# Causal mask of a maxima pass: added by a matrix product on TensorE, or by VectorE inside its maximum

## The chip, the cores and the metric

The kernel runs on one core of a Trainium2 chip. The metric is the device time of one execution in microseconds, as the median of several runs. The engines are called by their short names: PE is TensorE (PEld its weight loads), DVE VectorE, ACT ScalarE, POOL GpSimd, SP SyncE with its DMA queue (SPq).

## What is computed

The reference is one transformer decoder layer in float32, for 2 batches of 1024 tokens, 256 channels, 16 heads of 16 channels, and a context of 77 tokens:

```python
xn1 = _ln(x, g1, be1)
sa = _mha(xn1, xn1, Wq_s, bq_s, Wk_s, bk_s, Wv_s, bv_s, causal=True)
x = x + (sa @ W1 + b1)
xn2 = _ln(x, g2, be2)
ca = _mha(xn2, encoder_out, Wq_c, bq_c, Wk_c, bk_c, Wv_c, bv_c, causal=False)
x = x + (ca @ W2 + b2)
xn3 = _ln(x, g3, be3)
ff = jax.nn.relu(xn3 @ Wf1 + bf1) @ Wf2 + bf2
return x + ff
```

In `_mha` the scores are `q k^T / scale` with `scale = DH ** -0.5`, so they are multiplied by 4. In the causal attention the scores above the diagonal are set to minus infinity ahead of the softmax.

## The kernel before

**Stages.** The kernel normalizes x in four pieces of 512 rows, projects them to q, k and v, splits q and k into three bf16 parts each and stores these in DRAM. Then come the causal attention, its output product, the projection of the second q, the cross attention, its output product and the feed-forward part. This case is about the causal attention, some 65 to 350 us into the run.

**Groups.** The 2 x 16 heads are taken four at a time: 8 groups (NG), each with GH = 4 heads of one batch. A group goes through two passes over its scores.

**The maxima pass** finds the largest score of each query row, so that the exponential can be shifted. For a tile t of 128 queries the keys 0 to 128(t+1) are taken in chunks of up to 512 columns (`a.chunks`, a list of t, first head, number of heads, first key, width w). A chunk fills one PSUM bank of 512 float32 columns: four heads where w is 128, two where it is 256, one where it is 384 or 512. There are 38 chunks in a group. 22 of them hold the diagonal of their tile (`diagonal`, L906): 1, 2, 4 and 4 chunks for the widths 128, 256, 384 and 512, once for the tiles 0 to 3 and once more, from key 512 on, for the tiles 4 to 7. They hold 32 heads between them. PE fills a chunk with one matmul per head (L911). On a diagonal chunk a second matmul per head (L915) adds the mask to the last 128 columns: an identity in bf16 times `maskb`, which holds zeros and -1e30. DVE takes the maximum of each head with one reduce for the chunk (L1141) into `max_a`, or into `max_b` for keys from 512 on, and at the end of a group the larger of the two (L1146). POOL negates the 32 maxima per row and splits them into three bf16 parts (L600 to L609), PE transposes them (L922), DVE copies them to `shift_t` (L1154), and SP loads them as three further rows of the q stack (L428).

**The score pass.** PE computes the scores anew, transposed, and with the shift rows as part of the contraction (L948). ACT takes the exponential (L732), POOL zeroes the block above the diagonal (L617), and PE multiplies with v and a column of ones (L973; one product per step of key tiles). ACT copies the sums out and stores them, SP loads heads and sums back after every second group, DVE inverts the sums (L1169), SP spreads the inverses, and DVE multiplies (L1177).

**What sets the order.** Every engine runs its own list in order. `Attention.order` spreads the maxima chunks of a group between the score units of the group before it (`lead=1.35`: chunks are 1.35 groups ahead), so PE goes through chunks, score units, products and transposes in one list, `a.pe`, and the other engines follow the same list. The chunks rotate through three PSUM banks (`M_BANKS`): PE waits before chunk `use` until DVE has read chunk `use - 3` (`max_read`), DVE waits for `max_full`. The score units have three more banks, which ACT frees. The first 14 entries are run before the last projection, the next 30 are spread between its parts and the projection of the context.

Of the kernel before, what the change touches and what calls it, by code (L numbers as in the profile page):

```python
# [19 lines left out]
ALU = mybir.AluOpType  # L20
# [6 lines left out]
P = 128  # L27
# [167 lines left out]
def build(nc, x, w_qkv, w_ctx, w_mid, w_f1, w_f2, ctx_t, cols, rows, out):  # L195
# [12 lines left out]
    with ExitStack() as ctx:  # L208
        def sb(name, shape, dt=F32):
            return ctx.enter_context(nc.sbuf_tensor(name, shape, dt))  # L210
# [8 lines left out]
        row = sb("row", [P, 5, C])  # L219
        identf = sb("identf", [P, P])  # L220
        identb = sb("identb", [P, P], BF16)
        maskb = sb("maskb", [P, P], BF16)
        neghalf = sb("neghalf", [P, CT])

        arena_h = sb("arena_h", [P, NG // 2 * T])
# [16 lines left out]
        v_ctx = sb("v_ctx", [S_CTX, NG, GW])  # L242
        wf1_high = sb("wf1_high", [P, KC, FF], F32R)
        wf1r = (wf1_high[:, :, :], wf1_low[:, :, :])

        v_group = sb("v_group", [P, 3, TILES, GH, 32])
        out_t = sb("out_t", [P, T])
# [279 lines left out]
        def _(pool):  # L527
            c = [0]

            def made(ins, n=1):  # L530
                ins.then_inc(consts, 1)
                c[0] += 1
            made(pool.memset(identf[:, :], 0.0))
            made(pool.memset(identb[:, :], 0.0))
            made(pool.memset(maskb[:, :], 0.0))
            made(pool.memset(neghalf[:, :], -0.5))
            pool.wait_ge(consts, 4)
            for m in (identf, identb):
                made(pool.affine_select(out=m[:, :], in_=m[:, :], compare_op=ALU.not_equal, fill=1.0, base=0,
                                        pattern=[[-1, P]], channel_multiplier=1))  # L540
            made(pool.affine_select(out=maskb[:, :], in_=maskb[:, :], compare_op=ALU.is_ge, fill=NEG, base=0,
                                    pattern=[[-1, P]], channel_multiplier=1))

            def ln_root(k):

# [265 lines left out]
        def _(pe):  # L811
# [84 lines left out]
            def attention(a, s, lo, hi=None):  # L896

                def k_rows(n, g, h, lo, hi):
                    return (k_self[0:n, g % a.nb, h, lo:hi] if a.causal else k_ctx[0:n, g, h, lo:hi])

                def chunk(use, g, c):

                    t, h0, nh, s0, w = a.chunks[c]
                    if c == 0:
                        pe.wait_ge(s.q_in[g % a.nb], 16 * len(QP) * (1 + a.causal) * (g // a.nb + 1))
                        if g == 0 and not a.causal:  # L906
                            pe.wait_ge(s.k_in, 16 * len(KP))
                    diagonal = a.causal and s0 + w == (t + 1) * P
                    for h in range(h0, h0 + nh):
                        o = (h - h0) * w  # L910
                        ins = nc.tensor.matmul(m_bank(use)[:, o:o + w],  # L911
                                               q_stack[0:ROWS, g % a.nb, h, t * P:(t + 1) * P],
                                               k_rows(ROWS, g, h, s0, s0 + w), start=True, stop=not diagonal)
                        if diagonal:
                            ins = nc.tensor.matmul(m_bank(use)[:, o + w - P:o + w], identb[:, :], maskb[:, :],  # L915
                                                   start=False, stop=True)
                    return ins

                def shift_rows(use, g):
# [156 lines left out]
        def _(dve):  # L1076
# [55 lines left out]
            def attention(a, s, lo, hi=None):  # L1132

                def chunk(use, g, c):
                    t, h0, nh, s0, w = a.chunks[c]
                    p = g % 2
                    if c == 0:
                        at_least(dve, s.shift_step, 5 * (g - 2) + 1)
                        at_least(dve, s.maxima, g - 1)
                    dst = max_b[:, p, h0:h0 + nh, t - 4:t - 3] if s0 else max_a[:, p, h0:h0 + nh, t:t + 1]  # L1140
                    nc.vector.tensor_reduce(dst, m_bank(use)[:, 0:nh * w].rearrange("p (h w) -> p h w", h=nh),  # L1141
                                            AX.X, ALU.max).then_inc(s.max_read, 1)
                    if c + 1 == len(a.chunks):
                        dve.wait_ge(s.max_read, use + 1)
                        late = max_a[:, p, :, 4:8]
                        nc.vector.tensor_tensor(late, late, max_b[:, p, :, :] if a.causal else late, ALU.max)\  # L1146
                            .then_inc(s.maxima, 1)

                def shift_rows(use, g):
                    if g:  # L1150

                        dve.wait_ge(s.shift_in[(g - 1) % a.nb], 16 * PARTS * ((g - 1) // a.nb + 1))
                    src = m_bank(use).bitcast(BF16)[0:PARTS * GH * TILES, 0:P]
                    nc.vector.tensor_copy(shift_t[:, :], src).then_inc(s.max_read, 1)  # L1154

                def rows(use, n, half):

                    norm = (NCH if a.causal else 2 * NCH) + n
                    dve.wait_ge(bias_added, norm - NCH + 1)
                    add_half(m_bank(use).rearrange("p (j c) -> p j c", c=C), n, half).then_inc(s.max_read, 1)  # L1160
                    if half:
                        dve.wait_ge(s.max_read, use + 1)
                        ln_sums(norm)

                def invert_sums(g):
                    if g % 2 == 0:
                        return
                    dve.wait_ge(s.heads_in, 32 * (g // 2 + 1))
                    nc.vector.reciprocal(sums[:, :], sums[:, :]).then_inc(s.recips_done, 1)  # L1169

                def divide_heads(g):

                    if g % 2 == 0:
                        return
                    dve.wait_ge(s.recips_in, 16 * (g // 2 + 1))
                    o = heads_out[:, g // 2, :]
                    nc.vector.tensor_tensor(o, o, recips[:, :], ALU.mult).then_inc(s.heads_done, 1)  # L1177

                for op, *what in a.pe[lo:hi]:
                    if op == "score" and a.behind("inverted", *what) is not None:  # L1180
                        invert_sums(a.behind("inverted", *what))
                    if op == "score" and a.behind("divided", *what) is not None:
                        divide_heads(a.behind("divided", *what))
                    if op == "norm":
                        ln_apply((NCH if a.causal else 2 * NCH) + what[0])
                    if op != "m":
                        continue
                    use = what[0]
                    kind, *of = a.uses[use]
                    dve.wait_ge(s.max_full, use + 1)  # L1190
                    {"chunk": chunk, "shift": shift_rows, "rows": rows}[kind](use, *of)
                return invert_sums, divide_heads
# [10 lines left out]
            for n in range(3):  # L1203
                for u in range(4):
                    split(4 * n + u)
                add_v(n)
                if n == 0:
                    dve.wait_ge(x_in[3], 16)
                    ln_sums(3)
                    ln_apply(3)  # L1210
            attention(SELF, S1, 0, SELF_EARLY[0])
            for u in range(4):
                attention(SELF, S1, SELF_EARLY[u], SELF_EARLY[u + 1])
# [104 lines left out]
```

## Time and profile before

| | |
|---|---|
| median of 3 runs | 627.89 us |
| range of the runs | 627.78 to 629.59 us |
| span of the profiled execution | 631.5 us |
| busy share, PE / DVE / ACT / POOL | 80% / 58% / 49% / 30% |
| instructions, PE / DVE | 3296 / 695 |

The profile comes from an execution of its own, whose span stands in the table beside the timed runs. A busy share is an average over stages with different limits. The duration of a matmul is pipelined: its end overlaps the next one, so what a matmul costs is read from the distance of two starts. The same holds, to a lesser degree, for DVE.

### The profile page before, as it was taken

How to read it: one execution, taken by the hardware profiler on the slowest of the kernel's cores; microseconds unless marked ns; L12 is line 12 of the kernel's file. 1: busy time of each engine (PE TensorE's matmuls, PEld its weight loads, DVE VectorE, ACT ScalarE, POOL GpSimd, SP SyncE). 2: the span in 40 equal slices, each digit the busy share in tenths (PEclk: the TensorE clock that was granted, in tenths of full speed). 3: DMA queues.
4: the chain of work that ended last, by engine and by line, in shares of the span. 5: the costliest groups of instructions: out<-in, count | busy, mean ns of one | idle time of the engine just before them, and what ended most of it. 6: DMA issues, size and time to landing. Idle time of an engine off the chain costs nothing.

```text
span 631.5 us, 8807 instructions
## 1 busy us (share of the span) xinstructions
PE 504.7 (80%) x3296; PEld 296.2 (47%) x3296; DVE 368.2 (58%) x695; ACT 307.5 (49%) x590; POOL 187.8 (30%) x276
## 2 busy tenths in 40 slices
PE   1775775999997999799988835669576757989887
PEld 0664452344443444344333333434222446988877
DVE  4887697678886788678532147645221763454430
ACT  3544020667765776477666502247443535253460
POOL 3788821131221132122132523305131350121200
PEclk9988697799999999899999969767555968999998
DMA  8138936007367335727260266978333212101001
GB/s 288 47 109 158 201 116 118 0 21 116 52 120 105 67 66 107 115 56 38 83 186 1 68 168 92 173 108 140 107 99 115 81 47 72 34 0 34 18 17 34
DMA packets 41930, 56.51 MB, mean 89 GB/s; under 512 B 12832, under 2 KB 27424, under 8 KB 41888
## 3 DMA queue, kind: packets, MB, share of 16 engines
q1 hardware_dynamic: 39584, 47.56, 38.1%
q10 hardware_dynamic: 2304, 8.39, 3.8%
q8 instruction: 26, 0.43, 0.3%
q14 instruction: 16, 0.13, 0.1%
HBM read 35.12 MB, written 20.42 MB: 88 GB/s over the span
## 4 chain that ended last, share of the span: by engine, by line
PE 44%; DMA 23%; DVE 15%; ACT 6%; SPq 5%; issue 3%; POOL 2%; ACTq 0%; DVEq 0%
PE ps L864 10%; PE ps L973 9%; PE ps L948 8%; PE ps L911 7%; DMA arena_h<-heads 6%; DMA stacks<-shift_t 6%; PE ps L1060 5%; DMA recips<-recip_rows 4%; DVE max_a L1141 4%; ACT arena_p L732 4%; DMA heads<-out_t 4%; DVE xn L1094 3%; SPq L409 2%; PE ps L933 2%; SPq L428 2%
## 5 line engine op out<-in xcount | busy, mean ns | idle before, releaser
L732 ACT ACTIVATE arena_p<-ps 128x512 f32<-128x512 f32 (+4 forms) x416 | 190.9, 541 | 129.5 <-PE ps L948 127.3
L1141 DVE TENSOR_REDUCE max_a<-ps 128x1 f32<-128x512 f32 (+4 forms) x280 | 159.6, 620 | 46.6 <-PE ps L911 34.0
L948 PE MATMUL ps<-stacks 99*128 99x512 bf16 (+2 forms) x448 | 149.9, 369 | 27.6 <-DMA stacks<-shift_t 22.5
L911 PE MATMUL ps<-stacks 96*128 96x77 bf16 (+4 forms) x640 | 146.2, 306 | 32.1 <-DVE max_a L1141 19.1
L911 PEld LDWEIGHTS ps<-stacks 96*128 96x128 bf16 x640 | 58.9, 111 | 97.5 <-DVE max_a L1141 45.5
L973 PE MATMUL ps<-arena_p,v_group 128*32 128x512 f32 (+4 forms) x896 | 94.1, 540 | 0.7 <-POOL arena_p L617 0.5
L617 POOL TENSOR_SCALAR_AFFINE_SELECT arena_p<-arena_p 128x512 f32<-128x512 f32 x64 | 41.0, 653 | 169.9 <-ACT arena_p L732 169.9
L948 PEld LDWEIGHTS ps<-stacks 99*128 99x128 bf16 (+1 forms) x448 | 45.6, 107 | 93.1 <-ACT arena_p L732 37.8
L1141 DVE TENSOR_REDUCE max_b<-ps 128x1 f32<-128x384 f32 (+3 forms) x88 | 52.5, 636 | 21.3 <-PE ps L915 21.3
L864 PE MATMUL ps<-wf2r,hid_r 128*128 128x256 f32 x384 | 49.9, 294 | 9.6 <-DVE hid_r L1254 9.6
L864 PEld LDWEIGHTS ps<-wf2r,hid_r 128*128 128x128 f32 x384 | 49.1, 202 | 10.7 <-DVE hid_r L1254 10.7
L1121 DVE TENSOR_TENSOR xs<-ps,xs 128x512 f32<-128x512 f32 x24 | 16.4, 690 | 63.7 <-PE ps L864 44.7
L915 PE MATMUL ps<-maskb,identb 128*128 128x128 bf16 x256 | 51.9, 228 | 0.0
L1060 PE MATMUL ps<-xn_r,wf_high 128*128 128x512 f32 x128 | 42.3, 413 | 10.6 <-DVE xn_r L1247 10.6
L798 ACT ACTIVATE hid_r<-ps,col 128x512 fp32r<-128x512 f32 x32 | 22.1, 689 | 58.8 <-PE ps L1060 55.6
L571 POOL TENSOR_TENSOR parts<-arena_p,parts 128x512 bf16<-128x512 f32 (+1 forms) x26 | 32.2, 1239 | 39.2 <-DVE parts L1106 39.2
L717 ACT ACTIVATE arena_p<-ps,col 128x512 f32<-128x512 f32 (+1 forms) x26 | 17.3, 666 | 52.6 <-PE ps L848 43.2
L562 POOL TENSOR_TENSOR xs<-xs,row 128x256 f32<-128x256 f32 x48 | 38.6, 836 | 9.2 <-DVE xn L1094 9.2
L973 PEld LDWEIGHTS ps<-arena_p,v_group 128*32 128x32 f32 (+1 forms) x896 | 23.8, 112 | 36.2 <-issue 30.1
L1094 DVE TENSOR_SCALAR xn<-xs,mean_var,rstd 128x256 f32<-128x256 f32 x48 | 29.6, 678 | 16.7 <-POOL rstd L550 16.7
L1254 DVE TENSOR_TENSOR hid_r<-arena_p,hid_r 128x512 fp32r<-128x512 f32 x32 | 23.2, 731 | 19.8 <-ACT arena_p L801 19.8
L1104 DVE TENSOR_TENSOR arena_p<-arena_p,parts 128x512 f32<-128x512 f32 (+1 forms) x26 | 20.4, 785 | 24.0 <-issue 16.9
(68 smaller groups left out, 528.1 us busy)
## 6 DMA issues: line engine op xcount, KB each, us to landing
heads<-out_t ACTq DMA_DIRECT2D x16, 512.0 KB, 4.3
stacks<-q_parts SPq DMA_DIRECT2D x48, 128.0 KB, 5.2
stacks<-k_parts SPq DMA_DIRECT2D x48, 128.0 KB, 7.6
stacks<-qc_parts SPq DMA_DIRECT2D x48, 128.0 KB, 5.1
arena_h<-heads SPq DMA_DIRECT2D x8, 512.0 KB
recips<-recip_rows SPq DMA_DIRECT2D x8, 512.0 KB
q_parts<-parts SPq DMA_DIRECT2D x8, 384.0 KB, 2.5
k_parts<-parts SPq DMA_DIRECT2D x8, 384.0 KB, 2.6
```

The source lines that it names most:

```text
L562: ins = pool.tensor_tensor(xt, xt, row[:, r, :], ALU.add)
L571: pool.tensor_tensor(p[:, 2, :], rest[:, u % 2, 0:width], p[:, 1, :], ALU.subtract)\
L617: pool.affine_select(out=blk, in_=blk, compare_op=ALU.is_ge, fill=0.0, base=0, pattern=[[0, GH], [1, P]], channel_multiplier=-1).then_inc( ...
L732: nc.scalar.activation(probs[0:a.kp, a.probs_slot(g, ui), h, k * BANK:k * BANK + width], ps[0:a.kp, unit % S_BANKS, 0:width], ACT.Exp, sca ...
L864: ins = nc.tensor.matmul(acc[:, j, :], lhs_t(k, j), rhs(k), start=(k == 0), stop=(k == n_k - 1))
L911: ins = nc.tensor.matmul(m_bank(use)[:, o:o + w], q_stack[0:ROWS, g % a.nb, h, t * P:(t + 1) * P], k_rows(ROWS, g, h, s0, s0 + w), start=T ...
L915: ins = nc.tensor.matmul(m_bank(use)[:, o + w - P:o + w], identb[:, :], maskb[:, :], start=False, stop=True)
L948: ins = nc.tensor.matmul(ps[0:keys, unit % S_BANKS, lo - k * BANK:hi - k * BANK], k_rows(ROWS_S, g, h, i * P, i * P + keys), q_stack[:, g ...
L973: ins = nc.tensor.matmul(out_region[32 * h:32 * h + 32, lo:hi], v, probs[0:a.kp, slot, h, o:o + hi - lo], start=(i == 0), stop=last, skip_ ...
L1060: ins = nc.tensor.matmul(ps[:, 2 + u % 4, :], wf1r[hw][:, kc, f * P:(f + 1) * P], xn_r[:, hx, k % 2, kc, :], start=(i == 0), stop=(i == le ...
L1094: nc.vector.tensor_scalar(xn[:, p, j, :], xs[:, n * CT + j, :], mean_var[:, p, j, 0:1], rstd[:, p, j:j + 1], ALU.subtract, ALU.mult).then_ ...
L1141: nc.vector.tensor_reduce(dst, m_bank(use)[:, 0:nh * w].rearrange("p (h w) -> p h w", h=nh), AX.X, ALU.max).then_inc(s.max_read, 1)
```

## The change

The two matmuls per diagonal head become one. DVE reads the scores of one head from the bank and, from SBUF, a row of `w` mask values whose last 128 columns hold the triangle and whose others are zero. One fused instruction adds the two, writes the sum back to the bank and keeps the running maximum, which goes to `max_a` or `max_b`. There is one such instruction for each head of a diagonal chunk; the 16 other chunks of a group keep their single reduce. The semaphore `max_read` is raised by the last head of a chunk.

The mask is now float32, 128 x 512, and lies in the first 512 columns of `wf1_high`, a tile for the feed-forward weights that POOL fills near the end of the cross attention, long after the last causal chunk. POOL fills it with zeros at the start and writes the triangle into its last 128 columns. DVE waits once for these constants before its first chunk.

```diff
-        maskb = sb("maskb", [P, P], BF16)
...
+        mask_r = wf1_high[:, 0, 0:BANK]
+        mask = mask_r.bitcast(F32)
...
-            made(pool.memset(maskb[:, :], 0.0))
+            made(pool.memset(mask, 0.0))
...
-            made(pool.affine_select(out=maskb[:, :], in_=maskb[:, :], compare_op=ALU.is_ge, fill=NEG, base=0,
-                                    pattern=[[-1, P]], channel_multiplier=1))
+            made(pool.affine_select(out=mask_r[:, BANK - P:BANK], in_=mask[:, BANK - P:BANK], compare_op=ALU.is_ge,
+                                    fill=NEG, base=0, pattern=[[-1, P]], channel_multiplier=1))
...
-                    diagonal = a.causal and s0 + w == (t + 1) * P
...
-                                               k_rows(ROWS, g, h, s0, s0 + w), start=True, stop=not diagonal)
-                        if diagonal:
-                            ins = nc.tensor.matmul(m_bank(use)[:, o + w - P:o + w], identb[:, :], maskb[:, :],
-                                                   start=False, stop=True)
+                                               k_rows(ROWS, g, h, s0, s0 + w), start=True, stop=True)
...
-                    nc.vector.tensor_reduce(dst, m_bank(use)[:, 0:nh * w].rearrange("p (h w) -> p h w", h=nh),
-                                            AX.X, ALU.max).then_inc(s.max_read, 1)
+                    if a.causal and s0 + w == (t + 1) * P:
+
+                        for j in range(nh):
+                            ins = nc.vector.tensor_tensor_reduce(
+                                out=m_bank(use)[:, j * w:(j + 1) * w], in0=m_bank(use)[:, j * w:(j + 1) * w],
+                                in1=mask[:, BANK - w:BANK], scale=1.0, scalar=NEG, op0=ALU.add, op1=ALU.max,
+                                accum_out=dst[:, j, :])
+                        ins.then_inc(s.max_read, 1)
+                    else:
+                        nc.vector.tensor_reduce(dst, m_bank(use)[:, 0:nh * w].rearrange("p (h w) -> p h w", h=nh),
+                                                AX.X, ALU.max).then_inc(s.max_read, 1)
...
+            dve.wait_ge(consts, 7)
             attention(SELF, S1, 0, SELF_EARLY[0])
```

In the compiled program each fused instruction is two instructions of DVE: the pass itself and a read of its accumulator. This is DVE's list at the start of the causal attention, before (a row is a line, an operation, out<-in, the shape of the output and how often it repeats):

```order
L1114 TENSOR_TENSOR arena_v<-ps,row 128x4x64 x4
L1141 TENSOR_REDUCE max_a<-ps 128x4
L1141 TENSOR_REDUCE max_a<-ps 128x2 x2
L1141 TENSOR_REDUCE max_a<-ps 128x1 x12
L1141 TENSOR_REDUCE max_b<-ps 128x4
```

and in the changed kernel, where `wf_high` is the tile with the mask:

```order
L1111 TENSOR_TENSOR arena_v<-ps,row 128x4x64 x4
L1141 ISA ps,max_a<-ps,wf_high 128x128
L1141 ISA max_a 128x1
L1141 ISA ps,max_a<-ps,wf_high 128x128
L1141 ISA max_a 128x1
```

The one reduce of the first chunk has become four pairs, one per head. In the whole program DVE's list has 256 pairs in the place of 176 reduces.

On PE, at the same place (the end of the v projection and the first two chunks, for each of four heads), before:

```order
L864 MATMUL ps<-wqkv_r,xn_r 128x256 x24
L911 MATMUL ps<-stacks 128x128
L915 MATMUL ps<-maskb,identb 128x128
L911 MATMUL ps<-stacks 128x128
L915 MATMUL ps<-maskb,identb 128x128
```

and in the changed kernel:

```order
L865 MATMUL ps<-wqkv_r,xn_r 128x256 x24
L911 MATMUL ps<-stacks 128x128 x4
L911 MATMUL ps<-stacks 128x256 x4
L911 MATMUL ps<-stacks 128x384 x4
L911 MATMUL ps<-stacks 128x512 x7
```

The masks between the heads are gone, and with them the weight load of the identity and the weight load back to q, 256 times in the program. The order of everything else is the same on every engine.

## Rows read from the trace of the kernel before

**Rows 1.** The page: busy time, share and instructions of each engine.
```profile
PE 504.7 (80%) x3296; PEld 296.2 (47%) x3296; DVE 368.2 (58%) x695; ACT 307.5 (49%) x590; POOL 187.8 (30%) x276
```

**Rows 2.** Windows: length, busy us per engine (count), granted clock, DMA share, GB/s.
```profile
67.97:93.65 25.68, 21.42 (x117) 12.81 (x116) 24.98 (x46) 5.06 (x8) 12.79 (x5) 0.90 0.71 152
121.83:149.86 28.03, 28.00 (x227) 12.31 (x226) 22.54 (x42) 19.98 (x46) 6.72 (x14) 1.00 0.35 52
189.72:207.88 18.16, 14.30 (x109) 6.13 (x107) 12.13 (x20) 10.33 (x21) 2.74 (x5) 0.91 0.77 112
207.88:251.54 43.66, 43.52 (x346) 19.16 (x345) 35.05 (x63) 30.63 (x71) 10.70 (x24) 1.00 0.39 78
211.51:273.30 61.79, 57.64 (x452) 25.37 (x451) 47.10 (x84) 40.63 (x91) 13.44 (x28) 0.97 0.50 87
```

**Rows 3.** Chain of waits, 165 to 285 us: start, us, what.
```profile
183.16 6.54 DMA arena_h<-heads
...
193.66 7.77 DMA stacks<-shift_t
```

**Rows 4.** Waits of 120 to 322 us: total us, times, longest.
```profile
PEld ps L911 <- DVE max_a L1141: 16.4, 43, 0.8
```

**Rows 5.** Timeline of the plain group, PE's product, then DVE: start, us, engine, operation.
```profile
121.83 1.92 PE L973 MATMUL ps<-arena_p,v_group 128*32 128x512 f32 x16
...
124.11 1.02 DVE L1141 TENSOR_REDUCE max_b<-ps 128x1 f32<-128x384 f32 x2 [1.31 <-PE ps L915]
125.06 2.48 DVE L1141 TENSOR_REDUCE max_a<-ps 128x1 f32<-128x512 f32 x4
...
129.23 1.89 DVE L1141 TENSOR_REDUCE max_b<-ps 128x1 f32<-128x512 f32 x3 [1.10 <-PE ps L915]
131.15 0.18 DVE L1146 TENSOR_TENSOR max_a<-max_a,max_b 128x16 f32<-128x16 f32 x1
...
133.78 1.02 DVE L1141 TENSOR_REDUCE max_a<-ps 128x1 f32<-128x384 f32 x2 [0.64 <-PE ps L915]
...
138.48 1.89 DVE L1141 TENSOR_REDUCE max_a<-ps 128x1 f32<-128x512 f32 x3 [0.82 <-PE ps L915]
141.59 1.29 DVE L1141 TENSOR_REDUCE max_a<-ps 128x1 f32<-128x512 f32 x2 [1.22 <-PE ps L911]
...
146.23 1.29 DVE L1141 TENSOR_REDUCE max_b<-ps 128x2 f32<-128x512 f32 x2 [0.35 <-PE ps L915]
```

**Rows 6.** Groups by form: operation, shapes, count, busy us, mean ns, idle before.
```profile
L1141 DVE TENSOR_REDUCE max_a<-ps 128x1 f32<-128x512 f32 x160 | 100.7, 682 | 17.7 <-PE ps L911 12.6 <-PE ps L915 5.0
...
L915 PE MATMUL ps<-maskb,identb 128*128 128x128 bf16 x256 | 51.9, 228 | 0.0
...
L1141 DVE TENSOR_REDUCE max_b<-ps 128x1 f32<-128x384 f32 x32 | 16.2, 550 | 9.2 <-PE ps L915 9.2
```

**Rows 7.** Timeline of PE in that group: first of eight, and the next after.
```profile
130.13 0.22 PE L911 MATMUL ps<-stacks 96*128 96x128 bf16 x1
...
130.60 0.22 PE L948 MATMUL ps<-stacks 99*128 99x128 bf16 x1
```

**Rows 8.** Timeline of PE in the first chunk, a mask and what follows.
```profile
67.19 0.31 PE L915 MATMUL ps<-maskb,identb 128*128 128x128 bf16 x1
67.30 0.31 PE L911 MATMUL ps<-stacks 96*128 96x128 bf16 x1
```

**Rows 9.** Timeline of DVE, its smallest operations back to back; their group by form.
```profile
20.16 0.38 DVE L1085 BATCH_NORM_AGGREGATE mean_var<-stats 128x2 f32<-128x6 f32 x4
...
L1085 DVE BATCH_NORM_AGGREGATE mean_var<-stats 128x2 f32<-128x6 f32 x48 | 4.6, 157 | 0.4
```

**Rows 10.** Timeline of DVE and of SP's queue at the first shift rows.
```profile
102.07 0.21 DVE L1154 COPY shift_t<-ps 96x128 bf16<-96x128 bf16 x1
...
104.04 1.88 SPq L428 DMA_DIRECT2D stacks<-shift_t  x3
```

**Rows 11.** Timeline of POOL: its first work after the constants.
```profile
6.30 0.23 POOL L547 TENSOR_SCALAR veps<-mean_var 128x4 f32<-128x4 f32 x1 [2.63 <-DVE mean_var L1085]
```

## The prediction

> **What bounds the kernel now.** I first read the engine line of the page [rows 1]: PE 80%, DVE 58%. That average decides nothing, because the change touches only the causal attention, so I went to the windows of that stretch [rows 2]. They say three things. In the first chunks (67.97 to 93.65 us) DVE is busy 24.98 of 25.68 us: DVE sets the pace. In a plain group (121.83 to 149.86 us) PE is busy 28.00 of 28.03 us and DVE 22.54. Every second group is longer: 211.51 to 273.30 us is a pair of groups, 61.79 us, with 5.7 us more than two plain ones. I cut such a pair into a stall stretch (189.72 to 207.88 us in the pair before, 18.16 us) and a long stretch (207.88 to 251.54 us, 43.66 us, DVE busy 35.05). The chain of waits [rows 3] shows the stall stretch: a load of heads ends at 183.16 + 6.54 = 189.70 us, DVE must invert sums from it before it comes to the copy of the shift rows, the load of these rows takes 7.77 us, and PE scores again only when it has ended, at 193.66 + 7.77 = 201.43 us.
>
> So PE bounds the plain groups, with DVE at 80% behind it. The two are tied by three banks: in the waits of 120 to 322 us PE's chunk loads stand 16.4 us behind DVE's reduces [rows 4]. The DVE timeline of the plain group shows the other side [rows 5]: six waits for PE, 1.31, 1.10, 0.64, 0.82, 1.22 and 0.35 us, 5.44 in all. The PE row above them shows why: 16 product matmuls from 121.83 us take 1.92 us, PE fills no bank meanwhile, and DVE had 0.97 us of reduces left (it ran dry at 124.11 - 1.31 = 122.80 us).
>
> **What is removed.** A batch-head group has 8 x 4 = 32 diagonal heads, so 256 mask matmuls go, as many as the group table counts [rows 6]. Its 228 ns is a pipelined duration; from the start of the first to the end of eight such matmuls of 128 columns, four of them masks, go 130.60 - 130.13 = 0.47 us [rows 7], a step of 0.058 us. That is 32 x 0.058 = 1.86 us of PE per group, 14.9 us in all, and 0.11 us each where the granted clock is at its lower level [rows 8]. Also gone are the 22 reduces per group that read diagonal chunks.
>
> **What is added.** 32 fused passes per group, each two DVE instructions (the pass and a read of the accumulator). The elements stay: the same widths are read. What changes is the overhead per instruction. Four reduces of 512 take 2.48 us [rows 5], one lasts 0.682 [rows 6], so they start every (2.48 - 0.682) / 3 = 0.599 us. The forms of 384 and 512 differ by 0.682 - 0.550 us for 128 elements, about 1.04 ns each; 512 take 0.533 us of the step, and **0.066** is overhead. A group now pays 22 x 0.066 = 1.45 us for this.
> The pair's overhead, c, is in no row. Bounds: the four aggregates of 6 elements start every (0.38 - 0.157) / 3 = 0.074 us [rows 9]; if pass and read overlap like neighbours, c = 0.066 + 0.074 = **0.14**. If the read starts only after the pass has ended, as the small maximum at 131.15 does (0.03 us after the reduces' end at 129.23 + 1.89), c = 0.150 + 0.03 + 0.074 = **0.25** (0.150 is 0.682 less 0.533). Nothing excludes the low end and no semaphore stands between the two, which speaks for it; but the accumulator is whole only when the pass has gone through the pipe. I take half of that tail, **0.18**: per group 32 x 0.18 - 1.45 = +4.3 us of DVE.
>
> **The sum.** (1) First 16 heads, DVE bound: 16 x 0.18 - 11 x 0.066 = +2.15; the first reduce starts four mask matmuls earlier at the low clock, -0.43: **+1.7**. (2) Next 14 heads, among projections that also use DVE, before 95 us: 14 x 0.18 - 9 x 0.066 = **+1.9**. (3) Twelve heads before the shift copy at 102.07 us: +1.7, but the copy is over by 102.28 and SP issues the row loads only at 104.04, after the loads of the next stacks [rows 10]: 1.76 us of cover, **0**. Without that cover it would be +1.7. (4) A plain group: DVE 22.54 + 4.3 = 26.8 us, plus what is left of its waits. Where DVE is the later one, three full banks stand before it when a product starts: 3 x (1.02 - 0.55 + 0.115) = 1.75 us instead of 0.97, so 1.31 becomes 0.53 (0.115 is 0.18 - 0.066 a head); the other five, in the same way, about 0.56, 0.2, 0, 0.57, 0. Together 28.7 to 28.8 us against 28.03: **+0.75**, two groups **+1.5**. PE's saved 1.86 us is spent waiting for DVE. (5) A long stretch: 52 diagonal heads, 35 old reduces, 35.05 + 52 x 0.18 - 35 x 0.066 = 42.1, and 2.9 of waits, 45.0 against 43.66: +1.4; in its stall stretch two heads before the copy and four at the low clock: +0.3. Two pairs: **+3.4**. (6) The rest (111.56 to 121.83, and the last chunks behind 301.33 us): **+0.6**. Sum **+9.1 us**.
> At no cost: POOL fills 128x512 instead of 128x128, but it then stood idle 2.63 us for DVE's first statistics [rows 11]. The mask lies in a weight tile that is written after the last chunk. The new wait for constants on DVE is met 60 us before. ACT and the other DMAs keep their work and follow PE.
>
> A rule speaks against the change. The rows show reduces that start 0.599 us apart and last 0.682, so neighbours overlap by 0.083 us [rows 5, 6]. The Trainium skill, VectorE: DVE Perf Modes, "The DRAIN you can't avoid", says that the next operation waits until the pipe is empty. These rows do not bear that out for plain reduces; for the pair they cannot tell. What it would give is a rival below. The same page, "Two Vector instructions with no wait between them", counts an operation with an accumulator output as two instructions and holds neither when all operands start in the same quadrant of partitions, as here; by that the sum would be that of c = 0.14, and no run here shows it yet.
>
> **Rivals.** *Cheap pair, no net change.* c = 0.14: (1)+(2) +2.5, plain groups -0.5 each, pairs -0.6 each, total about 0: **628**. *Faster.* DVE stays off the path: the waits of rows 5 hide the added work, and PE cashes its matmuls: two plain groups -3.7, two long stretches with 52 masks -6.0, start +2.5: **621**. For it: 5.44 us of DVE idle per group, as much as is added. Against: they lie behind products, not spread out. It decides for c under about 0.155. *Costly pair.* c = 0.25: (1) to (3) +6.5, plain +3.0 each, pairs +5.6 each, rest +0.9: **652**. *Nothing overlaps.* The pass costs its whole duration and the read its own, c = 0.150 + 0.157 = 0.31: (1) to (3) +9.1, plain groups +9.8, pairs +17.8, rest +1.2: **666**. That is the time that the page's rule on the pipe gives. *Half speed.* The fused pass takes two cycles an element: 10,240 diagonal elements a group, 10.7 us more DVE in each: over **700**. Reduce and two-input operations both run one a cycle here, so little speaks for it.
>
> **How the numbers follow.** The sum is made against one profiled execution with a span of 631.5 us, 3.6 over the median of the runs, 627.89; the difference carries over: 627.9 + 9.1 = **637**. Chances: forecast (c 0.16 to 0.22) 0.46, costly 0.12, nothing overlaps 0.04, half speed 0.02, together 0.64 slower; cheap pair 0.17; faster 0.19. A measurement here tells 0.3%, 1.9 us, from no change. The forecast's own range is 631 to 645; with cases of both signs the range is 620 to 654, about one in ten outside it at either end.
>
> **What would show it.** In the changed profile: accumulator reads of about 0.07 to 0.16 us, and the step of a pair less its elements is c. If I am right DVE is busy about 27 of some 28.8 us in a plain group, its waits for PE shrink below 2.5 us, and PE's waits for DVE grow. DVE near 25 us and a group under 27.5 would prove me wrong towards faster; a c over 0.22 towards slower. If the start (to about 102 us) is not 3 to 4 us later, terms (1) and (2) are wrong.

## The result and the profile after

The changed kernel takes 636.05 us (median of 4 runs, 635.16 to 641.26), the kernel before, measured beside it, 628.74 (4 runs, 627.78 to 632.33). The ratio is 1.0133 [1.0067, 1.0199] (in brackets the 95% interval): slower, by 0.7 to 2.0%. A later comparison of the two (c_after below) gave 1.0102 [1.0046, 1.0158] (637.31 against 632.09 us). Ratios are formed from undisturbed runs, so they are not always the quotient of the medians beside them. Single runs of one kernel scatter by 5 us and more (the kernel before ran in 625.68 to 637.61 us on one chip), so what follows rests on lengths of stretches. The plain groups of a kernel repeat to 0.01 us and its start to 0.1 us; the stretch ahead of the first product and the stalled groups repeat less well, and are told with their scatter.

The profiled execution has a span of 633.5 us; its page:

```profile
span 633.5 us, 8632 instructions
...
PE 505.8 (80%) x3040; PEld 280.7 (44%) x3040; DVE 383.7 (61%) x1031; ACT 308.7 (49%) x590; POOL 187.7 (30%) x276
```

256 instructions less on PE, 336 more on DVE, and DVE's busy time is up by 15.5 us from 368.2 [rows 1]. The windows of the changed kernel, the first chunks up to the first projection matmul and the plain group, with the columns of [rows 2]:

```profile
66.22:74.42 8.20, 7.03 (x20) 2.00 (x20) 7.44 (x33) 0.00 (x0) 8.20 (x1) 0.50 1.11 237
123.40:151.86 28.46, 27.42 (x195) 10.09 (x194) 24.63 (x83) 20.31 (x45) 6.69 (x14) 1.00 0.36 52
```

And the same first stretch of the kernel before:

```profile
66.90:74.35 7.45, 7.03 (x35) 3.59 (x36) 6.38 (x12) 0.00 (x0) 7.45 (x1) 0.59 1.11 237
```

The plain group went from 28.03 to 28.46 us, DVE in it from 22.54 to 24.63 us, PE from 28.00 to 27.42. All four plain groups of the program have the same length, to 0.01 us, before and after. DVE's timeline of that group, its beginning and its waits for PE:

```profile
123.43 0.55 DVE L1141 CUSTOM_DVE_ANT_0 ps<-ps,wf_high 128x384 f32<-128x384 f32 x1
123.91 0.14 DVE L1141 DVE_READ_ACCUMULATOR2_ANT max_b<- 128x1 f32 x1
123.91 0.60 DVE L1141 CUSTOM_DVE_ANT_0 ps<-ps,wf_high 128x384 f32<-128x384 f32 x1
124.42 0.14 DVE L1141 DVE_READ_ACCUMULATOR2_ANT max_b<- 128x1 f32 x1
125.63 0.57 DVE L1141 CUSTOM_DVE_ANT_0 ps<-ps,wf_high 128x384 f32<-128x384 f32 x1 [1.07 <-PE ps L911]
...
130.69 0.70 DVE L1141 CUSTOM_DVE_ANT_0 ps<-ps,wf_high 128x512 f32<-128x512 f32 x1 [0.92 <-PE ps L911]
...
140.01 0.70 DVE L1141 CUSTOM_DVE_ANT_0 ps<-ps,wf_high 128x512 f32<-128x512 f32 x1 [0.36 <-PE ps L911]
...
143.12 1.29 DVE L1147 TENSOR_REDUCE max_a<-ps 128x1 f32<-128x512 f32 x2 [1.21 <-PE ps L911]
...
148.00 0.43 DVE L1141 CUSTOM_DVE_ANT_0 ps<-ps,wf_high 128x256 f32<-128x256 f32 x1 [0.24 <-PE ps L911]
```

Two things are to be seen. An accumulator read (0.14 us) starts at the same time as the next pass (both at 123.91): it does not hold that pass back. And the five waits are 1.07, 0.92, 0.36, 1.21 and 0.24 us, 3.80 in all, where [rows 5] had 5.44. How fast pairs follow each other is plain in the first chunk of 128 columns, four heads without a wait:

```profile
67.20 0.14 DVE L1141 DVE_READ_ACCUMULATOR2_ANT max_a<- 128x1 f32 x1
67.20 0.33 DVE L1141 CUSTOM_DVE_ANT_0 ps<-ps,wf_high 128x128 f32<-128x128 f32 x1
...
67.45 0.33 DVE L1141 CUSTOM_DVE_ANT_0 ps<-ps,wf_high 128x128 f32<-128x128 f32 x1
...
67.70 0.33 DVE L1141 CUSTOM_DVE_ANT_0 ps<-ps,wf_high 128x128 f32<-128x128 f32 x1
67.94 0.14 DVE L1141 DVE_READ_ACCUMULATOR2_ANT max_a<- 128x1 f32 x1
```

One pair every 0.248 us (67.20 to 67.45 to 67.70 us). The groups by form say what each part lasts:

```profile
L1147 DVE TENSOR_REDUCE max_a<-ps 128x1 f32<-128x512 f32 x128 | 80.9, 682 | 12.4 <-PE ps L911 12.3
...
L1141 DVE CUSTOM_DVE_ANT_0 ps<-ps,wf_high 128x512 f32<-128x512 f32 x64 | 43.1, 717 | 8.6 <-PE ps L911 8.6
...
L1141 DVE DVE_READ_ACCUMULATOR2_ANT max_b<- 128x1 f32 x128 | 18.0, 140 | 0.0
...
L1141 DVE CUSTOM_DVE_ANT_0 ps<-ps,wf_high 128x128 f32<-128x128 f32 x64 | 16.6, 322 | 4.3 <-PE ps L911 4.3
```

Pairs on 128, 256, 384 and 512 columns start every 0.248, 0.382, 0.516 and 0.650 us. That is a line with 1.047 ns for an element, and what it leaves for no elements, 0.248 - 128 x 0.001047, is **c = 0.114 us**.

The waits from 120 to 322 us:

```profile
DVE ps L1141 <- PE ps L911: 19.7, 27, 1.3
...
PEld ps L911 <- DVE max_b L1141: 18.5, 37, 0.8
PEld ps L911 <- DVE max_a L1147: 13.3, 38, 0.5
PEld ps L911 <- DVE max_a L1141: 12.2, 24, 0.9
```

The row of [rows 4] is only one of two in the kernel before; the other, for the reduces into `max_b`, is

```profile
PEld ps L911 <- DVE max_b L1141: 6.9, 11, 0.8
```

So PE's chunk loads stood 16.4 + 6.9 = 23.3 us behind DVE before, and now stand 18.5 + 13.3 + 12.2 = 44.0 us. A plain group is longer than before although PE has 1.86 us less to do in it: all that PE saved, and 0.43 us more, goes into waiting.

### The profile page after: what moved, and what is told of

The parts are those of the page before. It is cut to its first block, busy times and chain, and to the rows that moved or that the text cites. A ratio compares the mean times of both kernels' runs of the same rounds, so it can differ in the third digit from the quotient of the medians.

```text
span 633.5 us, 8632 instructions
## 1 busy us (share of the span) xinstructions
PE 505.8 (80%) x3040; PEld 280.7 (44%) x3040; DVE 383.7 (61%) x1031; ACT 308.7 (49%) x590; POOL 187.7 (30%) x276
## 4 chain that ended last, share of the span: by engine, by line
PE 42%; DVE 24%; DMA 20%; SPq 4%; ACT 4%; issue 3%; POOL 2%; ACTq 0%; DVEq 0%
PE ps L865 10%; PE ps L970 8%; DVE ps L1141 7%; PE ps L911 7%; PE ps L945 7%; DMA stacks<-shift_t 6%; DVE max_a L1147 5%; PE ps L1057 5%; DMA recips<-recip_rows 4%; DMA arena_h<-heads 4%; DVE xn L1091 3%; ACT arena_p L733 2%; PE ps L930 2%; SPq L429 2%; SPq L410 2%
## 5 line engine op out<-in xcount | busy, mean ns | idle before, releaser
L945 PE MATMUL ps<-stacks 99*128 99x512 bf16 (+2 forms) x448 | 152.5, 374 | 26.3 <-DMA stacks<-shift_t 21.2
L911 PE MATMUL ps<-stacks 96*128 96x77 bf16 (+4 forms) x640 | 142.3, 309 | 34.0 <-DVE max_a L1147 14.8
L1141 DVE CUSTOM_DVE_ANT_0 ps<-ps,wf_high 128x128 f32<-128x128 f32 (+3 forms) x256 | 117.9, 520 | 24.0 <-PE ps L911 23.9
L1147 DVE TENSOR_REDUCE max_a<-ps 128x1 f32<-128x512 f32 (+1 forms) x192 | 109.6, 613 | 36.1 <-PE ps L911 35.9
L911 PEld LDWEIGHTS ps<-stacks 96*128 96x128 bf16 x640 | 55.5, 111 | 120.5 <-DVE max_a L1147 32.2
L865 PE MATMUL ps<-wf2r,hid_r 128*128 128x256 f32 x384 | 48.6, 290 | 8.4 <-DVE hid_r L1261 8.4
L1118 DVE TENSOR_TENSOR xs<-ps,xs 128x512 f32<-128x512 f32 x24 | 16.4, 689 | 63.3 <-PE ps L865 44.3
L865 PEld LDWEIGHTS ps<-wf2r,hid_r 128*128 128x128 f32 x384 | 47.8, 198 | 9.6 <-DVE hid_r L1261 9.6
L1057 PE MATMUL ps<-xn_r,wf_high 128*128 128x512 f32 x128 | 42.5, 414 | 10.6 <-DVE xn_r L1254 10.6
L1261 DVE TENSOR_TENSOR hid_r<-arena_p,hid_r 128x512 fp32r<-128x512 f32 x32 | 23.3, 730 | 20.2 <-ACT arena_p L802 20.2
L548 POOL TENSOR_SCALAR veps<-mean_var 128x4 f32<-128x4 f32 x12 | 2.7, 228 | 104.6 <-DVE mean_var L1082 104.5
```

The lines of the kernel that those rows point to most:

```text
L865: ins = nc.tensor.matmul(acc[:, j, :], lhs_t(k, j), rhs(k), start=(k == 0), stop=(k == n_k - 1))
L911: ins = nc.tensor.matmul(m_bank(use)[:, o:o + w], q_stack[0:ROWS, g % a.nb, h, t * P:(t + 1) * P], k_rows(ROWS, g, h, s0, s0 + w), start=T ...
L945: ins = nc.tensor.matmul(ps[0:keys, unit % S_BANKS, lo - k * BANK:hi - k * BANK], k_rows(ROWS_S, g, h, i * P, i * P + keys), q_stack[:, g ...
L1057: ins = nc.tensor.matmul(ps[:, 2 + u % 4, :], wf1r[hw][:, kc, f * P:(f + 1) * P], xn_r[:, hx, k % 2, kc, :], start=(i == 0), stop=(i == le ...
L1141: ins = nc.vector.tensor_tensor_reduce(out=m_bank(use)[:, j * w:(j + 1) * w], in0=m_bank(use)[:, j * w:(j + 1) * w], in1=mask[:, BANK - w: ...
```

## Experiments

Each kernel is told as a diff against the changed kernel, and measured against the kernel before on the same chip. "Group" is a plain group; its length and DVE's busy time in it are read from windows. The plain groups of a run agree within 0.02 us, those of e6, e8 and e11 within 0.09 us.

Two theories were put up. **A**: PE and DVE hold each other up through the three banks, so work on either lengthens the group by a part of itself. **B**: PE sets the group and cashes all that it is relieved of, and the changed kernel loses time only where the pairs of a narrow chunk hold a bank long.

**e1_no_mask: PE's saving alone.** DVE has its plain reduces back and PE's mask matmuls stay out. The kernel leaves out the mask of the maxima pass altogether, so the maxima are taken over later keys as well; the block above the diagonal is still zeroed behind the exponential.

```diff
-                    if a.causal and s0 + w == (t + 1) * P:
-
-                        for j in range(nh):
-                            ins = nc.vector.tensor_tensor_reduce(
...
+                    nc.vector.tensor_reduce(dst, m_bank(use)[:, 0:nh * w].rearrange("p (h w) -> p h w", h=nh),
+                                            AX.X, ALU.max).then_inc(s.max_read, 1)
```

> The PE part of the change alone: the 256 mask matmuls are left out and DVE keeps its plain reduces, so the maxima pass runs without a causal mask at all. Theory A (PE and DVE are tied by the three banks, so neither can cash what it saves alone): a plain group goes from 28.03 to about 27.3 us, because DVE's 22.5 us and at least 4.5 us of waits behind the products stay; the kernel gains 5 to 6 us. Theory B (PE is the bound, and the changed kernel loses time only where four accumulator pairs of a narrow chunk hold a bank long): PE cashes all of its 1.86 us, a plain group takes 26.2 us, the kernel gains about 13 us.

**e2_both: DVE's addition alone.** The mask matmuls come back, the fused passes stay.

```diff
+        maskb = sb("maskb", [P, P], BF16)
...
+                    diagonal = a.causal and s0 + w == (t + 1) * P
...
+                        if diagonal:
+                            ins = nc.tensor.matmul(m_bank(use)[:, o + w - P:o + w], identb[:, :], maskb[:, :],
+                                                   start=False, stop=True)
```

> The DVE part of the change alone: the fused passes of the changed kernel, and PE adds its mask too (so the diagonal blocks are masked twice). Theory A: DVE's 2.1 us more per group are partly hidden by its waits, a plain group takes about 29.2 us, the kernel is some 10 us slower than before. Theory B: PE's blocked time of the changed kernel (0.43 + 1.86 = 2.3 us a group) is added in full, a plain group takes 30.3 us, the kernel is about 17 us slower than before. In both, if it was the missing masks that kept TensorE's clock at its lower level in the first chunks, the first six projection matmuls behind them (2.56 us in the changed kernel) take 1.65 us again, as before.

**e3_wide and e4_narrow: the change for half of the heads.** e3 fuses the 16 heads of a group with 384 or 512 columns and masks the others on PE; e4 does the reverse. The diff is DVE's side of e3; PE's side is that of e2 with `and w < 3 * P`.

```diff
-                    if a.causal and s0 + w == (t + 1) * P:
+                    if a.causal and s0 + w == (t + 1) * P and w >= 3 * P:
```

> The change for chunks of 384 and 512 columns only (one head, so one accumulator pair per chunk); narrow diagonal chunks keep the PE mask and the plain reduce. DVE gets 16 x (0.114 - 0.066) = 0.8 us more per group, PE loses 0.93 us. Theory A: a plain group takes 27.6 to 28.0 us, the kernel is within 3 us of before, on the faster side. Theory B: no bank is held by a burst of pairs, PE cashes its masks, a plain group takes 27.1 us, the kernel is 5 to 6 us faster than before.

> The other half: fused passes for chunks of 128 and 256 columns only (four or two pairs per chunk); wide diagonal chunks keep the PE mask and the plain reduce. DVE gets 16 x 0.114 - 6 x 0.066 = 1.4 us more per group, PE loses 0.93 us. Theory A: a plain group takes about 28.4 us. Theory B: all of the changed kernel's loss and only half of PE's gain, 28.03 + 2.3 - 0.93 = 29.4 us.

Measured, one plain group of e1, e2, e3 and e4:

```profile
123.26:150.47 27.21, 27.05 (x194) 10.18 (x193) 22.54 (x41) 19.66 (x45) 6.72 (x14) 1.00 0.35 51
```

```profile
123.03:152.10 29.07, 28.45 (x226) 12.09 (x226) 24.64 (x84) 20.55 (x45) 6.72 (x14) 1.00 0.36 52
```

```profile
153.11:180.91 27.80, 27.54 (x211) 11.31 (x210) 23.31 (x57) 19.91 (x46) 6.72 (x14) 1.00 0.50 80
```

```profile
123.83:152.39 28.56, 27.86 (x211) 11.04 (x210) 23.84 (x68) 20.39 (x45) 6.72 (x14) 1.00 0.36 51
```

| kernel | median, us | ratio to before | group, us | DVE busy, us |
|---|---|---|---|---|
| before | | | 28.03 | 22.54 |
| e1_no_mask | 631.10 | 0.9935 [0.9891, 0.9978] | 27.21 | 22.54 |
| e2_both | 641.49 | 1.0171 [1.0119, 1.0222] | 29.07 | 24.64 |
| e3_wide | 634.58 | 1.0058 [1.0024, 1.0092] | 27.80 | 23.31 |
| e4_narrow | 637.21 | 1.0096 [1.0058, 1.0135] | 28.56 | 23.84 |
| changed | 636.05 | 1.0133 [1.0067, 1.0199] | 28.46 | 24.63 |

B had 26.2, 30.3, 27.1 and 29.4 us for the groups of e1 to e4, A had 27.3, 29.2, 27.6 to 28.0 and 28.4: B falls on all four; A stands. Nor does the longer engine alone set the group: that would leave e2 at the 28.03 us of before. As whole kernels e1 gained 0.65% or 4 us (5 to 6 were expected) and e2 lost 1.7% or 11 us. Nor is it the missing masks alone that keep the clock of the start low: with the masks back on PE (e2) the first six projection matmuls last 2.85 us. Those of the changed kernel, put at 2.56 us in the expectation, last 3.07 by the trace.

A gives prices. Without the masks PE has 1.86 us less to do, and the group is 0.82 us shorter: 0.44 us for each us of PE; where DVE has its passes already (e2 to the changed kernel) the same work gives back 0.61 us, 0.33 for each. With DVE's 2.10 us more the group is 1.04 longer (0.50 for each), and where the masks are gone already (e1 to the changed kernel) 1.25 longer (0.60). Wide heads are the better half: they had a reduce of their own, so a pair in its place costs DVE 0.114 - 0.066 = 0.048 us and saves PE 0.058; e3's group is 0.23 us under before. A narrow head had a half or a quarter of a reduce; e4's is 0.53 over. The two prices do not explain all of this: with DVE's busy time from the table (+0.77 and +1.30 us) and 0.93 us less of PE they give e3 no change and e4 +0.2 to +0.4. So it also counts where in the list the work lies, and several pairs on one bank seem to cost more than one; no run separates this. Yet e3 as a whole was slower than before, by 0.6% [0.2, 0.9], where the expectation had it on the faster side. That pointed to the start of the attention.

e1 is the only one of these that is faster than before as a whole. Softmax does not depend on the shift so long as the exponentials stay in range, so the mask of this pass guards the range and not the value; whether it may be left out hangs on the size of the scores, and this case does not settle that.

**c_before and c_after: the two kernels again.** They are unedited.

> The kernel before once more, unchanged, as a control for the first chunks and the stalls. Plain groups take 28.03 us again. If the granted clock's rise in the first chunks belongs to the kernel, the first six projection matmuls behind them take 1.65 us as in the first look; if it differs from execution to execution, they may take up to 3 us here too, and that part of the loss is no effect of the change.

> The changed kernel once more, unchanged, as a control on the same chip as the next three. Plain groups of 28.46 us. If the late rise of the granted clock in the first chunks belongs to the kernel, the first six projection matmuls behind them take over 2.5 us again, where two looks at the kernel before gave 1.65 us; from the first chunk's first matmul to SP's first issue of shift rows 39.9 us, against 37.1. The time is 5 to 9 us over that of the kernel before.

c_before: 632.08 us, ratio 1.0003 [0.9975, 1.0032]. c_after: 637.31 us, 1.0102 [1.0046, 1.0158], group 28.46 again. The groups that hold a stall lasted, in the two profiles of each kernel, 33.62, 33.76, 34.16 and 33.3 us before and 35.43, 33.01, 35.87 and 33.84 after: means 33.71 and 34.54, +0.8 us each with a scatter of 1 to 2 us.

**e5_slope: a known addition to DVE, which missed.** Each pair gets a memset of one column behind it.

```diff
+                            nc.vector.memset(spare[:, spared[0]:spared[0] + 1], 0.0)
```

> The changed kernel with one more tiny DVE instruction behind every accumulator read (it fills one unused column; the bank is handed back before it). It prices DVE time alone: 32 x about 0.07 = 2.2 us per group, which lifts the pair's overhead from 0.114 to about 0.18, the value of the forecast. Forecast's own arithmetic for that value: a plain group of 28.8 us. Theory A with the waits as measured (3.8 us of them stay): each us of DVE costs a half to two thirds, a plain group takes 29.5 to 30.0 us. If DVE is already the only bound: the whole 2.2 us, 30.7 us.

The group took 28.55 us, +0.09, with DVE busy 24.79: pairs with a memset start every 0.25 us instead of 0.248. The memset is recorded inside the next pass and costs next to nothing, where 0.07 us was expected. The +0.09 us for +0.16 of DVE is too small to be a price; the whole time, 638.84 us, 1.0097 [1.0062, 1.0131], is that of the changed kernel.

**e11_all_fused: the addition that e5 was to be.** The 16 other chunks get pairs too, with zeros for a mask.

```diff
-                    if a.causal and s0 + w == (t + 1) * P:
+                    if a.causal:
+                        row_m = mask[:, BANK - w:BANK] if s0 + w == (t + 1) * P else zeros
```

> The changed kernel with the other 16 chunks of a causal group fused as well (they add a row of zeros): DVE time alone, PE's list untouched, 16 x (0.114 - 0.066) = 0.8 us more per group. Theory A (both count about half): a plain group goes from 28.46 to 28.8 to 28.9 us. If DVE alone is the bound by now: 29.2 us. If PE alone is: 28.46 us.

```profile
123.74:152.77 29.03, 27.82 (x194) 9.95 (x193) 25.62 (x99) 20.43 (x45) 6.69 (x14) 1.00 0.37 55
```

DVE +1.0 us (0.8 was expected, 16 x (0.114 - 0.066)), group 29.03, +0.57: again some 0.6 for each us of DVE, and between the 28.46 us that was expected for a PE bound and the 29.2 for a DVE bound. Time 640.68 us, 1.0158 [1.0102, 1.0213].

**e6_banks and e8_wide_banks: four banks for the maxima.** The fourth is taken from the score units, which keep two; e8 is e6 with the masks of e3.

```diff
-                    at_least(pe, s.exps, unit - S_BANKS + 1)
+                    at_least(pe, s.exps, unit - (2 if a.causal else S_BANKS) + 1)
...
-                        at_least(pe, s.max_read, use - M_BANKS + 1)
+                        at_least(pe, s.max_read, use - M_BANKS - m_late(a, use) + 1)
```

> The changed kernel with four PSUM banks for the maxima chunks and two for the scores once the projections are done (before: three and three). Theory A (the three banks tie PE and DVE): with a fourth, DVE has a further chunk to work on while PE runs a product, its waits fall from 3.8 us to under 2 us a group, and a plain group goes from 28.46 to 26.5 to 27.5 us, unless ACT with only two score banks becomes the bound. Rival (the length of a group is set by something else, say ACT's exponentials or the order of the list): no gain, or a loss, 28.4 us or more.

> The wide-chunk version with the same four and two banks. Theory A: below its 27.80 us per plain group, to 26 to 27 us, and faster than the kernel before by 5 to 10 us. Rival: 27.8 us or more.

The waits of e6 from 120 to 322 us:

```profile
PEld ps L953 <- ACT arena_p L741: 80.3, 183, 0.9
```

Groups of 31.4 and 31.5 us, where A had 26.5 to 27.5 and 26 to 27 us; times of 658.53 (1.0415 [1.0373, 1.0458]) and 657.70 us (1.0409 [1.0364, 1.0453]). PE's loads now wait 80.3 us for ACT to free a score bank. This says that the scores need their third bank; what a fourth bank would do for the maxima it does not say, since the two edits came together.

**e10_two_banks: one bank less for the maxima, the scores as they were.**

```diff
+            if m_late(a, use):
+                return ps[:, S_BANKS + (U0 + (use - U0) % 2) % M_BANKS, :]
...
-                        at_least(pe, s.max_read, use - M_BANKS + 1)
+                        at_least(pe, s.max_read, use - M_BANKS + m_late(a, use) + 1)
```

> The changed kernel with two banks instead of three for the maxima chunks, once the projections are done; the scores keep their three. Theory A (the banks tie PE and DVE): DVE has one chunk less in hand when a product starts, each of six waits grows by up to 0.6 us, and PE waits more often for a free bank: a plain group goes from 28.46 to 30.5 us or more, the kernel is 12 us or more slower than the changed one. Rival (the length of a group is set by the score side, as it was with only two score banks): 28.5 to 29 us.

```profile
125.23:158.03 32.80, 28.88 (x195) 9.30 (x194) 25.14 (x84) 21.49 (x45) 6.74 (x14) 1.00 0.35 50
```

32.80 us a group, where the rival had 28.5 to 29; 655.77 us, 1.0410 [1.0358, 1.0462]. With the same work on both engines the number of banks alone is worth 4.34 us of a group. That is the tie that A speaks of.

**e9_late_wide: e3 with group 0 left as before.** `g` is the group; PE keeps its masks for all of group 0.

```diff
-                    if a.causal and s0 + w == (t + 1) * P:
+                    if a.causal and s0 + w == (t + 1) * P and w >= 3 * P and g:
```

> The wide-chunk version from the second group on; the first group is as in the kernel before. The start costs nothing then (first projection matmuls 1.65 us, shift rows issued 37.1 us after the first chunk's start), and five plain groups and the others gain 0.23 us each: 626 to 632 us where the kernel before has its 628 to 632, a gain of 0 to 2 us. If the start's loss has another cause than the work of the first group, it stays, and the kernel is 2 to 4 us slower than before.

Its plain group is e3's, 27.81 us, and its start is that of before. Its time is 629.04 us, 0.9972 [0.9940, 1.0005] of the kernel before and 8.3 us under the changed kernel on the same chip. Of the versions that keep the mask of this pass it is the best, though not clearly faster than before. The first six matmuls of the projection after the first chunks, in this kernel, in the changed one and in the kernel before (start, us, operation):

```profile
73.27 1.68 PE L853 MATMUL ps<-xn_r,wqkv_r 128*128 128x512 f32 x6
```

```profile
74.42 3.07 PE L849 MATMUL ps<-xn_r,wqkv_r 128*128 128x512 f32 x6
```

```profile
74.35 1.65 PE L848 MATMUL ps<-xn_r,wqkv_r 128*128 128x512 f32 x6
```

The same six matmuls take 3.07 us in the changed kernel and 1.65 to 1.68 us where group 0 is as before. In all three profiled executions with that group 0 (1.65, 1.65, 1.68) the clock had risen before the projection; in all eleven with something changed there it had not, or only in part (2.53 to 3.07). Among these are e2, which keeps the mask matmuls, and e1, which keeps the reduces. The granted clock says the same: 0.59 over the stretch ahead of the projection before, 0.50 after, which is the lower level, 1.2 GHz, throughout (the windows above).

The moment of the rise also moves between executions of one kernel. The mask matmuls show it, first in the kernel before and then in c_before, the same kernel:

```profile
72.39 0.31 PE L915 MATMUL ps<-maskb,identb 128*128 128x128 bf16 x1
72.93 0.26 PE L915 MATMUL ps<-maskb,identb 128*128 128x128 bf16 x1
```

```profile
69.27 0.31 PE L915 MATMUL ps<-maskb,identb 128*128 128x128 bf16 x1
69.76 0.22 PE L915 MATMUL ps<-maskb,identb 128*128 128x128 bf16 x1
```

Counted from the first chunk's first matmul, the granted clock goes from 0.50 to 1.00 after 6.1, 3.3 and 5.4 us in the kernel before, c_before and e9, and after 9.5 to 12.7 us in the eleven others. The two sets lie apart by more than either scatters, so the late rise belongs to the edits. One thing goes with it: ahead of the rise PE has no idle time in the three, while in each of the eleven it stands idle for 0.1 to 1.0 us within the first 4 us, when weight loads wait for DVE to free a bank. That this is the cause is not shown.

e3 and e9 differ in group 0 alone: SP issues the shift rows 39.40 us after the first chunk's first matmul in e3 and 37.17 us after it in e9, against 37.13 and 37.14 us before and 39.94 and 40.05 us in the changed kernel. e1 tells what the clock alone is worth there: it has less work on PE and the same on DVE, and still issues them after 38.05 us, +0.9.

## Why the prediction was right, and where it was not

The forecast was 637.0 us, +9.1; measured were 636.05 us, which by the ratios is 0.0133 x 628.7 = +8.4 and, in the later comparison, 0.0102 x 632.1 = +6.4 us. The traces add up to less: start, up to the issue of the shift rows, +2.8, four plain groups 4 x 0.43 = +1.7, two stalled groups +1.7, the stretch from scores to first product -0.6, the last groups -0.15, together +5.4 us. The intervals on the ratios (+4.2 to +12.5 and +2.9 to +10.0 us) hold that sum, as does the scatter of the stalled groups and loads. So the side was right and the size is within the noise of the runs; that 637.0 lies so near 636.05 is partly luck, since the parts that can be traced make +5.4 and not +9.1, and two of the terms came near by errors that cancel.

**c, chosen as 0.18: 0.114 measured.** The step that failed is "I take half of that tail". The measured c lies even under the prediction's lower bound of 0.14. That bound added a separate small operation, 0.074, to a reduce's overhead of 0.066; the rows show the read starting together with the next pass, so only 0.114 - 0.066 = 0.048 us comes on top. DVE gained 2.1 us a group (32 x 0.114 - 1.45 = 2.2), not 4.3. The Trainium skill, VectorE: DVE Perf Modes, "Two Vector instructions with no wait between them", is right for this pair in that the read is not held back (both at 123.91 us). The prediction took c = 0.31 and 666 us from "The DRAIN you can't avoid" on the same page; it left out that this section itself lets a next operation that is not held start earlier. Measured were 0.114 and 636 us.

**Term (4), waits of 1.9 us left beside 26.8 of DVE: 3.8 beside 24.6.** 26.8 + 1.9 = 28.7 and 24.6 + 3.8 = 28.4 are nearly the same sum, so a group's +0.75 came out as +0.43 by luck as much as by the mechanism. The waits' step assumed three full banks before DVE when a product starts, 1.75 us of reading. The rows show 1.16: DVE's reading ends at 124.56 (125.63 - 1.07), and the product started at 123.40. With c = 0.114 three full banks would be 1.55. But DVE's last reduce of 512 ends at 123.43, 0.03 us behind the product's start, so of three banks the oldest was all but read by then and DVE had two in hand. A DVE that runs with less slack still runs dry behind every product.

**The threshold, "decides for c under about 0.155": wrong.** c is well under it and the kernel is slower. The rival took DVE's 5.44 us of waits for a reserve that new work fills. e1, e2 and e11 show that none of the work is free: DVE's costs the group 0.5 to 0.6 of itself and PE's gives back 0.33 to 0.44, so +2.1 and -1.86 us come out at a loss though they are nearly equal. Half of my test for "faster" came true (DVE near 25 us) and the other half did not (28.46 us, not under 27.5). DVE's waits were to shrink below 2.5 us; they are 3.8. That PE would wait more for DVE is right, 23.3 to 44.0 us in all; the prediction's 16.4 was one of two rows.

**Terms (1) and (2), +3.6 us: +2.8, but of other parts.** With c = 0.114 they come to about +0.8 and +1.0 (16 x 0.114 - 11 x 0.066, less the 0.31 us by which the first pass starts earlier; 14 x 0.114 - 9 x 0.066). The remaining +1.0 was not in the sum at all. The six projection matmuls at the lower clock last 1.42 us longer, and DVE stands 1.84 us for them, where it stood 0.28 us before (and 1.92 us in e1, whose start is 0.9 us longer with no work added):

```profile
77.85 0.69 DVE L1147 TENSOR_REDUCE max_a<-ps 128x1 f32<-128x512 f32 x1 [1.84 <-PE ps L911]
```

I had taken the clock as it stood in the trace of before and not asked whether other work ahead of its rise would move the rise. By the prediction's own test (3 to 4 us later) the two terms just fail.

**Term (3), nothing: right.** The copy and the load of the shift rows in the changed kernel:

```profile
105.04 0.22 DVE L1160 COPY shift_t<-ps 96x128 bf16<-96x128 bf16 x1
```

```profile
106.16 1.86 SPq L429 DMA_DIRECT2D stacks<-shift_t  x3
```

The copy ends at 105.26, the issue follows at 106.16: 0.90 us of cover are left of 1.76.

**Term (5), +3.4 for two pairs: about +2.5** (two plain groups of +0.43 and two stalled ones of +0.8). c was too large in it as well, and the stalled groups scatter by more than the error. **Term (6), +0.6: -0.75.** The stretch between the first scores and the first product took 10.3 and 10.6 us in the two profiles of the kernel before and 9.6 and 10.0 in those of the changed one; the last groups are 0.15 us shorter. I had the sign wrong. But most of the 0.6 us is not work: 5.8 and 6.6 us of the stretch lay at the lower level of the clock before, 4.8 and 5.5 us after, and 1.1 us less at half speed is worth 0.5 us. In e5, whose PE work is that of the changed kernel, the clock rose after 6.0 us and the stretch took 10.3 us, as before. So this part is the scatter of the clock, and about 0.1 us is left for the matmuls that are gone.

**What stays open.** What decides when the clock rises in the first chunks was not isolated: runs with less PE work, with more DVE work and with both moved it. PE's pause ahead of the first chunk was also longest in the three executions with an early rise (9.69 to 10.08 us, against 8.40 to 9.75); the nearest two, e9 with 9.69 and e5 with 9.75 us, speak against the pause as the cause, with matmuls of 1.68 and 3.07 us, but no run varied it. A fourth bank for the maxima with three left to the scores was not tried.

## What to carry to other kernels

Where two engines hand work to each other through a few banks, the longer one doesn't set the time alone: price both sides, here 0.33 to 0.44 us back for each us taken from the feeder and 0.5 to 0.6 us paid for each us given to the consumer, and move only the instructions that cost the consumer less than they save the feeder (here the wide heads, 0.048 us against 0.058). Idle time of the consumer behind a burst of other work on the feeder hides only part of what is added, here 0.4 to 0.5 of it. An edit in the first us after a pause can also shift the rise of TensorE's clock: look at a stretch that the edit does not touch, such as the projection here, before its cost is put down to the edit, and look at more than one execution, since the rise moves between executions too.

## What was unexpected in the hardware

- The accumulator read of a fused pass starts with the next pass and lies inside it; a pair on 512 columns takes 0.650 us, 0.051 more than a reduce of the same elements, though its two records last 0.72 + 0.14 us against 0.68.
- A one-column memset behind each pair added 0.002 to 0.005 us to its step (e5).
- The fused pass, which reads PSUM and SBUF and writes PSUM in place, goes at 1.047 ns an element, as the reduce does at about 1.04.
- Six identical matmuls took 1.65 us in the kernel before and 3.07 us in the changed one, because TensorE's clock had risen ahead of them in the one and not in the other; each of the edits of the first group, on either engine, put the rise later (9.5 to 12.7 us after the first chunk's first matmul, against 3.3 to 6.1).
